# Attention of a four-layer gated cross-attention network: fillers at the turned maxima, column scores by fours, projections among the row scores

## The reference

```python
# L0 and L3 cross-attention, 16 heads of 8; L1's second one, 16 heads of 32
scores = jnp.einsum('bhqd,bhkd->bhqk', qh, kh) * scale
attn = jax.nn.softmax(scores, axis=-1)
out = jnp.einsum('bhqk,bhkd->bhqd', attn, vh)
# L1's first one ("a1"): self-attention, 16 heads of 32, the part t > s kept after the softmax
q = jnp.einsum('bsc,hcd->bhsd', xn, wq)
k = jnp.einsum('btc,hcd->bhtd', yn, wk)
v = jnp.einsum('btc,hcd->bhtd', yn, wv)
# L1 feed-forward ("l1f"): self-attention of 16 heads of 8, scores of later tokens set to 0,
# softmax over all, then a router that sends each token to one of 8 experts
att = jnp.where(tril, att, 0.0) / jnp.sqrt(jnp.float32(d))
```

## Time and profile before

| | |
|---|---|
| timed runs | 1976.22, 1944.81, 1953.66 us; median 1953.66 |
| the profiled execution | 1932.59 us, its span 1930.5 us |
| granted TensorE clock, mean | 0.870 of full speed |
| TensorE busy | 1643.6 us, 85% of the span |
| VectorE, ScalarE, GpSimd busy | 880.0, 715.9, 146.9 us |

### The profile page before, as it was taken

The page is one execution under the profiler, slowest core; times in us unless marked ns, Lnnn a source line. Parts: engine busy times, 40 slices in busy tenths (PEclk is TensorE's granted clock), DMA queues, the critical chain, the costliest instruction groups (busy, mean ns, idle before and its releaser), DMA issues.

```text
span 1930.5 us, 22528 instructions
## 1 busy us (share of the span) xinstructions
PE 1643.6 (85%) x9068; PEld 762.3 (39%) x9068; DVE 880.0 (46%) x1746; ACT 715.9 (37%) x1267; POOL 146.9 (8%) x207
## 2 busy tenths in 40 slices
PE   5748999989899989997648999989899989988487
PEld 2323333332344536633323323332343436543274
DVE  4474664253456353324474663353456352337312
ACT  2333455324435225232332455323445125243133
POOL 0000011100012000000000111100012000002232
PEclk9768899989989699956768999989999689889688
DMA  4000000000000100000000000000000100002241
GB/s 178 1 1 0 1 2 1 1 1 1 0 1 1 44 1 1 1 1 2 1 1 0 1 1 1 0 1 1 0 1 2 44 1 1 1 33 44 62 135 59
DMA packets 18107, 30.17 MB, mean 16 GB/s; under 512 B 4640, under 2 KB 12640, under 8 KB 17104
## 3 DMA queue, kind: packets, MB, share of 16 engines
q1 hardware_dynamic: 16752, 26.10, 4.2%
q0 software_dynamic: 1248, 2.59, 0.4%
HBM read 23.49 MB, written 5.19 MB: 15 GB/s over the span
## 4 chain that ended last, share of the span: by engine, by line
PE 78%; DVE 12%; ACT 7%; issue 2%; DMA 1%; SPq 0%; POOL 0%; POOLq 0%; DVEq 0%; ACTq 0%
PE ps L783 8%; PE ps L881 5%; PE ps L670 5%; PE ps L613 3%; PE ps L815 3%; PE ps L1323 3%; PE ps L1335 3%; PE ps L1020 3%; PE ps L695 3%; PE ps L1012 3%; PE ps L932 2%; PE ps L829 2%; PE ps L1242 2%; PE ps L912 2%; PE ps L804 2%
## 5 line engine op out<-in xcount | busy, mean ns | idle before, releaser
L2000 DVE TENSOR_REDUCE peak<-ps 128x1 f32<-128x512 f32 x256 | 165.4, 686 | 119.0 <-PE ps L783 118.4
L1620 ACT ACTIVATE big<-ps 128x512 f32<-128x512 f32 x256 | 139.6, 595 | 133.8 <-PE ps L806 126.9
L783 PE MATMUL ps<-pp,qT 32*128 32x512 f32 x512 | 169.5, 714 | 3.5 <-DVE peak L2000 2.1
L804 PE MATMUL ps<-qT,pp 32*128 32x512 f32 x512 | 160.4, 649 | 0.0
L1641 ACT ACTIVATE big<-ps 128x512 f32<-128x512 f32 (+3 forms) x256 | 100.3, 436 | 112.5 <-PE ps L912 111.7
L2037 DVE TENSOR_REDUCE crest<-ps 128x2 f32<-128x512 f32 (+3 forms) x128 | 105.2, 825 | 65.7 <-PE ps L887 65.6
L1574 ACT ACTIVATE big<-ps 77x1024 f32<-77x1024 f32 x96 | 94.7, 1019 | 95.8 <-PE ps L670 95.2
L912 PE MATMUL ps<-qT,pp 32*128 32x256 f32 (+3 forms) x512 | 124.4, 494 | 0.9 <-ACT big L1641 0.9
L1927 DVE TENSOR_REDUCE small<-ps 128x8 f32<-128x616 f32 x96 | 74.2, 797 | 102.8 <-PE ps L641 58.1
L881 PE MATMUL ps<-pp,qT 32*128 32x384 f32 (+3 forms) x512 | 109.2, 501 | 9.5 <-DVE crest L2037 8.5
L1555 ACT ACTIVATE sq<-ps 128x512 f32<-128x512 f32 x52 | 31.1, 597 | 204.4 <-PE ps L613 204.4
(11 more groups left out here) (484 smaller groups left out, 2775.3 us busy)
## 6 DMA issues: line engine op xcount, KB each, us to landing
big<-in_w SPq DMA_DIRECT2D x23, 256.0 KB
pt<-in_l2w SPq DMA_DIRECT2D x2, 2048.0 KB, 7.5
w_l<-in_l SPq DMA_DIRECT2D x1, 3086.0 KB, 17.3
pp<-in_w SPq DMA_DIRECT2D x1, 2048.0 KB, 9.6
big<-by_expert SPq DMA_DIRECT2D x23, 66.0 KB, 2.0
by_expert<-cst SPq DMA_DIRECT2D x1, 1472.0 KB, 16.3
cst<-in_const SPq DMA_DIRECT2D x1, 1298.0 KB, 5.8
w_l<-in_l SPq DMA_DIRECT2D x1, 1218.0 KB, 8.0
```

The costliest lines, as they stand in the source:

```text
L783: pe.matmul(rbank(x), qT[at, u, k, 128 * i:128 * i + 128], keyT(u, k)[at, :], start=True, stop=True, tile_position=(32 * c, 0)).then_inc(* ...
L804: pe.matmul(tbank(y), keyT(u, k)[at, 128 * j:128 * j + 128], qT[at, u, k, :], start=True, stop=False, tile_position=(32 * c, 0))
L1620: A(prob(m)[:, TURN_OF[g], :], tbank(tplace(m, g)), ACT.Exp).then_inc(*SCALAR.did("a1", "exp", m, g))
L2000: v.tensor_reduce(peak[:, p // 4 % 2, i, c:c + 1], rbank(ring(p, c)), AX.X, ALU.max)\
```

## The change

Three things. In `cross`, bf16 matmuls of 512 columns whose result nobody reads (`busy`) stand around both `turned`, and with dh = 8 two of them behind each of the eight row score steps of u = 0; and the column scores of two steps are issued together (`colscores4`: four float32 matmuls, then four bf16 ones), for u = 1 everywhere and for u = 0 with dh = 32, where the ring's places follow. In `attend`, the 24 projections are cut into groups among the first row scores, use banks 0, 1, 6 and 7, and are all evicted by ScalarE; the row scores use four banks there. In `attend_past`, the turned maxima and what raises q by them come half a step later, the end steps for u = 0 come earlier and those for u = 1 later, among the routing.

```diff
+            def busy(b, n):
+                for _ in range(n):
+                    pe.matmul(PSB[b], identb[:], w1q[:], start=True, stop=True)
...
                 def turned(u):
-                    x = cplace("turned", u)
+                    x = cplace(dh, "turned", u)
+                    free(x)
+                    busy(cbank(x) + 1, 4)
                     pe.wait_ge(*VECTOR[tag, "cut", u])
-                    free(x)
                     for i in range(4):
...
                     mm.then_inc(*TENSOR.did(tag, "turned", u))
+                    busy(cbank(x) + 1, 4)
...
+                def colscores4(u, k):
+                    for less in (False, True):
+                        for a in (2 * k, 2 * k + 1):
+                            for b in (0, 1):
+                                colscore(u, a, b, less)
...
                 for a in range(8):
                     rowscores(0, a)
+                    if dh == 8:
+                        busy(0, 2)
                 turned(0)
-                for a in range(8):
-                    colscores(0, a)
-                    rowscores(1, a)
+                for k in range(4):
+                    if dh == 8:
+                        for a in (2 * k, 2 * k + 1):
+                            colscores(0, a)
+                            rowscores(1, a)
+                    else:
+                        colscores4(0, k)
+                        rowscores(1, 2 * k)
+                        rowscores(1, 2 * k + 1)
...
                 for p in range(5):
+                    project(range(max(0, 5 * p - 1), 5 * p + 4))
                     for c in range(4):
                         rowscore(p, c)
...
+                    if n in (0, 12):
+                        pe.wait_ge(*VECTOR["a1 in", u])
+                    if n >= 4:
+                        pe.wait_ge(*SCALAR["a1 made", n - 4])
...
-                    if m == 28:
+                    if m == 26:
                         pe.wait_ge(*VECTOR["l1f", "max", 31, 1])
                         spread_out("e0", 0, 1)
-                    if m == 29:
-                        spread_out("e0", 1, 2)
                         heads(0, 0)
                         heads(0, 1)
+                    if m == 29:
+                        spread_out("inv", 0, 4)
+                    if m == 30:
+                        spread_out("e0", 1, 2)
                     if m == 31:
-                        spread_out("inv", 0, 4)
-                    if m == 32:
-                        heads(1, 0)
-                heads(1, 1)
-                logits(0)
-                spread_out("inv", 1, 2)
+                        logits(0)
...
                 turned_hot(0)
+                heads(1, 0)
+                heads(1, 1)
```

More of the change, by code:

```diff
@@ L736, in cross @@
                 turned(1)
-                for a in range(8):
-                    colscores(1, a)
-                    if a >= 3 and a % 2:
-                        sums(1, (a - 3) // 2)
-                        values(1, (a - 3) // 2)
+                for k in range(4):
+                    colscores4(1, k)
+                    if k:
+                        sums(1, k - 1)
+                        values(1, k - 1)
                 if dh == 8:
@@ L938, in heads @@
                 def heads(u, hf):
-                    bank = 3 - 2 * u
-                    pe.wait_ge(*(VECTOR["l1f", "raised", 7] if u == 0 else VECTOR["l1f", "later", 0]))
+                    bank = (2, 7)[u]
+                    pe.wait_ge(*(VECTOR["l1f", "max", 31, 1] if u == 0 else SCALAR["l1f", "exp", 31, 3]))
                     pe.wait_ge(*SCALAR["l1f", "kept", 2 * u + hf])
@@ L976, in attend_past @@
                             values(m - 2)
+                        if g == 2 and m % 4 == 3 and m < 28:
+                            turned((m + 1) // 4)
                         if m + 6 < 32:
@@ L2034, in maxima @@
                     for h in (0, 1):
+                        if h and p % 4 == 1 and p > 1:
+                            raised(p // 4 - 1)
                         b = pbank(pplace(p, h))
```

208 lines of the change are left out of this document (104 added, 104 removed).

## The result

| | before | changed |
|---|---|---|
| median of the runs | 1950.55 us (1944.81 to 1976.22, 4 runs) | 1915.04 us (1913.02 to 1918.95, 4 runs) |
| profiled execution, its span | 1932.59, 1930.5 us | 1913.02, 1911.2 us |
| granted clock, mean | 0.870 | 0.882 |
| forecast | | 1895 us (1858 to 1926) |

The ratio is 0.9882, with a 95% interval from 0.9832 to 0.9931: 1.2% less time, where 3.0% was forecast. Equal times lie outside the interval, but the gain is under the 2% that the prediction asked of a change before it calls it faster. The ratio goes by fast executions alone (slow is more than 1.5% above a kernel's fastest), so it is not the quotient of the two medians, 0.982. The kernel before ran from 1917 to 1989 us in the series of this study, the changed one from 1907 to 1919 in its eight runs. So a part of what the change does seems to be that it no longer has the long runs.

The account below looks back on a forecast made before the run. TensorE was taken as the bound, busy for 85% of the span and often below full clock. Six parts summed to -52 us from 1932.59, giving 1880.5; 15 us carried from the median's excess made 1895 us, range 1858 to 1926.

Parts of the forecast that it names:

- Part 1: Four dh=8 crosses: fillers close the wait at `turned(0)`, column scores keep full clock; -21.3 us, between -24 and 0.
- Part 2: Cost of the fillers in the crosses, behind row scores and around turned maxima: +14.5 us, from +6 to +20.
- Part 3: Column scores by fours, u=0 with dh=32: 3.64 us instead of 4.92 for two steps, -10.3 us in all.
- Part 4: Projections among the first row scores in `attend`: first column score 11.5 us earlier, -23.0 us, between -27 and -17.
- Part 5: Loop of l1f: turning half a step later halves TensorE's 0.56 us wait; -4 us, between 0 and -8.
- Part 6: End of l1f and routing: same work reordered, -4 us a turn, -8 us; between -30 and +6.
- The scale: Median lies 21 us above the profiled execution; 15 us of it carried, turning 1880.5 into 1895 us.
- A: Rival: the fillers don't hold the clock in the crosses and are paid partly at half speed; 1921 us, chance 0.17.
- B: Rival: the routing's clock stays up too, part 6 is -30 instead of -8; 1873 us, chance 0.11.
- C: Rival: projections run cold at the head of `attend`; 1941 us, 1955 to 1965 if the loop behind is cold; chance 0.05.
- D: Rival: parts 3 and 4 are hidden by another engine, such as ScalarE's order; 1905 us, chance 0.09.
- The rule: Clock set by TensorE's recent busyness: it would return by itself in all four crosses, part 1 worth little, about 1913 us.

Follow-up runs that it names:

- series 1: Changed kernel with l1f's old order 1912.17 us; without row score fillers 1886.42; without any filler 1891.93; with twelve fillers around l1f's heads steps 1883.78.
- series 3: Changed kernel with l1f's u=0 end block late 1889.89 us; fillers moved 1868.69; moved, old l1f order 1892.24; moved, more fillers behind dh=8 heads steps 1861.45.
- series 4: Kernel with moved fillers, l1f's u=0 end block late and filled, 1868.72 us; changed kernel with only heads steps, inv and logits late, 1901.11 us.

## Why the prediction was wrong, point by point

The sum of the prediction was made on the scale of the profiled execution, and there it can be held against the trace:

| part | forecast, us | in the trace, us |
|---|---|---|
| 1. clock in the dh = 8 crosses | -21.3 | -23.6 |
| 2. fillers | +14.5 | +23.6 |
| 3. column scores by fours | -10.3 | -10.2 |
| 4. projections | -23.0 | -19.4 |
| 5. loop of l1f | -4 | -0.9 |
| 6. end of l1f, routing | -8 | +5.6 |
| the rest, by difference | 0 | +5.3 |
| sum | -52 | -19.6 |

The rest is the stretches between those that the change touches, +5.0 from norm to norm, the first matmuls of the mlp ahead of l1f, +3.4 (below), and the other parts of the crosses, some -3.

**Part 1 was right in its size**, but its reason is only half right. I put the fall down to the wait for the maxima. In the second cross the clock was down before that wait began at 821.3 us, with TensorE still in its row scores:

```profile
820.50:821.25 0.75, 0.75 (x4) 0.00 (x0) 0.75 (x2) 0.00 (x0) 0.00 (x0) 0.53 0.00 0
```

It was the same in the fourth cross (0.60 from 1684.00 to 1684.60 us, TensorE busy throughout); in the third it fell as the wait began, and only in the first 1.4 us behind its end. So closing the wait is not what kept the clock up in all four; that the fillers as a whole did so is shown (all 28 crosses with dh = 8 in the seven profiles with the full set are at 1.00 through these stretches, and each of the 16 in the four profiles with none has a fall), which of them and why is not. That it was worth 23.6 us rests on the profiled execution, whose second cross was cold to its end. Without any filler the same stretches had 6 us less to give.

**Part 2 was mis-sized**, the term of the fillers behind the row scores. I took 0.53 us for the two tiles of a row score step and VectorE as the pace of 0.72. The 0.53 came from one full-array row score, where a step here is a thin pair; in the changed kernel that pair takes 0.72 by itself, so TensorE had no gap for the fillers, and they add 0.53 a step: from the first row score to the first column score it was 8.31 us in the first cross and is 12.18, +3.87 instead of +2.0 (with the turned maxima +2.1). The other three took 8.5 us before, so four crosses make +14.8; the fillers ahead of `turned(1)` are +0.86 each, +3.4; with dh = 32 they cost 2.7 a turn (series 1), where I had 1.1. The sum is 23.6. The filler itself costs what I took: 0.215 us.

**Part 3 was right** to 0.1 us: 28.24 us from transposes to transposes became 24.00, with 0.86 of fillers in it, so 5.1 a turn.

**Part 4 was right in its mechanism**. The head is 10.6 us shorter (11.5 forecast). Over the whole self-attention it is 10.9 in the first turn and 8.5 in the second.

**Part 5 failed small.** The wait of 0.56 us is gone, but from the first to the last maxima of the loop it is 0.54 us less in the first turn and 0.37 in the second. The period of four m went from about 12.49 to 12.37 us; what sets it now I did not pursue.

**Part 6 is the step that failed**, the largest miss of the sum, 13.6 us. I wrote "the work is not less, only in another order" and took 4 us a turn of gain. Behind the last maxima of the loop the changed kernel takes 2.7 us more in the first turn and 2.9 in the second. My other case in that part, that "the block of small matmuls at m = 26 puts the clock down three m earlier", priced at +3 a turn, is what happened, in its direction and nearly in its size. I gave it no chance of its own; it should have been a rival. Putting the block back late (series 3) and putting fillers around it (series 1) both undo that, by 8 and 13.6 us a turn. What stayed open is which of the small steps does it, if any one does (series 4).

**The scale.** I carried 15 of the 18 to 21 us between the profiled execution and the median into the changed kernel. Only 2.0 were left: 1915.04 against 1913.02. The changed kernel's runs lie close together. The sum was 32.5 us off; the 13 us from the scale go the other way and cover a part of that, and so the time lies inside the range. That is luck: the nearness of 1915 to 1895 says nothing for the working.

**The rivals.** A (the fillers don't hold the clock) had the nearest time, 1921, and is refuted: all four stretches are at 1.00. B (the routing's clock stays up) did not happen; the kernel with fillers in l1f comes nearest to it, with 13.5 us at half, at 1884 with the costly fillers still in. C and D are refuted: the projections ran at full clock from the fifth on, and ScalarE's evictions made TensorE wait 0.69 us only.

**The rule.** In the kernel without fillers the clock was down in each cross, with TensorE busy for 91 to 96% of the stretch, and came back within it; in the second cross of the kernel before it did not in 26 us at 99% busy. The Trainium skill (TensorE: Matmul & The Clock Gate, Part 1) sets the gate by how busy the engine has recently been. That the clock came back in the first four stretches agrees with that; the last one does not, nor does the fall with TensorE busy (part 1), if busy is what the profile shows. By the rule I had put part 1 at a few us; with and without fillers the four stretches differ by 13.7.

## What to carry to other kernels

Where fillers stand decides what they are worth: here 12 of them around small steps in l1f, at full clock, gave 13.6 us a turn; eight around the turned maxima of the dh = 8 crosses paid too, though the clock was often down when they came; and 16 behind row scores cost 3.85 us a cross and can have saved 2.2 at most. Before a block of small matmuls is moved earlier, look at what the clock does behind it in the trace; here it went with a loss that was larger than what the order gained. And a term that comes from one profiled execution's cold stretch should be set against the spread of the runs: a kernel that ranges over 72 us has a clock that takes different paths.

## What the runs showed of the hardware

The granted clock does not follow from the instruction order alone. The l1f stretch took 208.87 us in the first and 214.96 us in the second turn of one execution; the kernel before took from 1916.78 to 1989.23 us in one series. The full-array float32 matmuls behind a wait of 3.03 us in the mlp ahead of l1f ran at full clock in the kernel before and at 0.80 in the changed one:

```profile
484.00:492.70 8.70, 8.66 (x17) 3.80 (x18) 0.55 (x1) 4.79 (x7) 0.00 (x0) 0.80 0.00 0
```

Before, the same work took 6.97 us at 1.00, here 8.65. A full-array bf16 matmul of 512 columns costs 0.215 us between starts at full clock and 0.415 at half (four in 0.86 and in 1.66 us), and a dozen of them, behind a fall and with small steps between, did not lift the clock again; eight around the transposes in the kernel without row score fillers did (down at 39.0 us, up at 42.3).
